# A staged fp32 transformer block on one core: in its ball stage the spread of reciprocal row sums goes to the end of a step, column scalings go to ScalarE, and a widening copy goes to GpSimd

## The reference

```python
def plin(x, w, b):                 # linear map between ball points
    return expmap0(logmap0(x) @ w + b)

xm = expmap0(layer_norm(logmap0(x)) * (1 + sc_msa) + sh_msa)
q, k, v = heads(plin(xm, w_q, b_q)), ...          # 16 heads of 16
attn = softmax(q @ k.T / sqrt(16))
attn_out = plin(from_heads(expmap0(attn @ v)), w_o, b_o)
x = mobius_add(residual, expmap0(g_msa * logmap0(attn_out)))
xm = expmap0(layer_norm(logmap0(x)) * (1 + sc_mlp) + sh_mlp)
ff = plin(plin(xm, w_f1, b_f1), w_f2, b_f2)       # 256 -> 1024 -> 256
out = mobius_add(x, expmap0(g_mlp * logmap0(ff)))
```

## Time and profile before

| what | us |
|---|---|
| median of 3 runs (range) | 3740.58 (3738.3 to 3744.46) |
| the profiled execution: its own time | 3737.99 |
| its span, first to last instruction | 3736.2 |
| stage 1, up to | 1205 |
| ball stage | 1205 to 2213 |
| of it, attention (first to last scores) | 1280.6 to 2067 |
| stage 3 | 2213 to 3736 |

### The profile page before, as it was taken

How to read it: one execution, slowest core, us unless ns; L and a number is a source line. 1 busy time by engine, 2 the same in 40 slices (tenths; PEclk the granted TensorE clock), 3 DMA queues, 4 the chain that set the end, 5 groups by cost and what they waited for, 6 DMA issues and landing times. The chain is left out here.

```text
span 3736.2 us, 51318 instructions
## 1 busy us (share of the span) xinstructions
PE 3404.0 (91%) x18088; PEld 1908.1 (51%) x18088; DVE 2195.9 (59%) x6472; ACT 1645.3 (44%) x3155; POOL 378.1 (10%) x234
## 2 busy tenths in 40 slices
PE   8999999999984588988898758999999999999998
PEld 3555555555552233444444434555555555555554
DVE  3234333334344567677775647777777777777773
ACT  2333333333331255544445215655555555555552
POOL 0000000000001001111112211111111111111110
PEclk9999999999997799999999879999999999999999
DMA  4010110110002100000000030000000000000000
GB/s 164 33 57 32 38 57 32 37 60 29 32 12 88 38 5 8 9 13 14 12 9 12 11 127 17 23 21 21 20 21 21 21 23 26 26 27 28 21 27 20
DMA packets 77553, 120.48 MB, mean 32 GB/s; under 512 B 10313, under 2 KB 66532, under 8 KB 72050
## 3 DMA queue, kind: packets, MB, share of 16 engines
q1 hardware_dynamic: 77298, 117.20, 9.1%
HBM read 96.16 MB, written 16.83 MB: 30 GB/s over the span
## 5 line engine op out<-in xcount | busy, mean ns | idle before, releaser
L2569 PE MATMUL wps<-w_wqkv,w_hT 128*128 128x512 f32 x768 | 379.4, 618 | 3.1 <-DMA w_wo<-in_wwo 3.1
L2607 PE MATMUL wps<-w_xnT,w_w 128*128 128x512 f32 (+1 forms) x768 | 351.5, 598 | 24.5 <-DVE w_xnT L2432 20.3
L2191 POOL TENSOR_TENSOR w_rn<-w_n,w_mhalf 128x16 f32<-128x16 f32 x64 | 187.4, 2927 | 1096.9 <-DVE w_n L2369 1096.9
L2219 ACT ACTIVATE w_pr<-w_sm,w_nmx,w_rn 128x256 f32<-128x256 f32 (+1 forms) x512 | 286.4, 562 | 10.2 <-DVE w_nmx L2350 9.6
L603 PE MATMUL ps<-xT,rw 128*128 128x512 f32 x512 | 245.4, 602 | 0.0
L2607 PEld LDWEIGHTS wps<-w_xnT,w_w 128*128 128x128 f32 (+1 forms) x768 | 133.2, 178 | 217.3 <-issue 193.7
L619 PE MATMUL ps<-hid,rw 128*128 128x512 f32 x512 | 240.7, 592 | 0.0
L1290 ACT ACTIVATE bb_pr<-bb_ps 128x1024 f32<-128x1024 f32 x128 | 130.5, 1020 | 203.8 <-PE bb_ps L1800 203.5
L2206 ACT ACTIVATE w_pT<-wps 128x512 f32<-128x512 f32 (+1 forms) x128 | 69.6, 544 | 329.2 <-PE wps L2516 329.2
L2569 PEld LDWEIGHTS wps<-w_wqkv,w_hT 128*128 128x128 f32 x768 | 137.9, 193 | 132.8 <-issue 127.7
L2619 PE MATMUL wps<-w_w,w_h2T 128*128 128x256 f32 (+1 forms) x768 | 190.1, 392 | 1.8 <-issue 1.8
(11 more groups left out here) (318 smaller groups left out, 6594.3 us busy)
## 6 DMA issues: line engine op xcount, KB each, us to landing
rw<-in_ew SPq DMA_DIRECT2D x32, 1024.0 KB, 6.7
w_xa<-xs SPq DMA_DIRECT2D x16, 512.0 KB, 3.8
w_xin<-xs SPq DMA_DIRECT2D x64, 128.0 KB, 3.8
xT<-in_xT SPq DMA_DIRECT2D x8, 512.0 KB, 3.9
xres<-in_x SPq DMA_DIRECT2D x32, 128.0 KB, 2.2
x<-x1t SPq DMA_DIRECT2D x32, 128.0 KB, 1.7
b_x<-x SPq DMA_DIRECT2D x1, 4096.0 KB, 14.3
bb_mod<-ada SPq DMA_DIRECT2D x16, 256.0 KB, 3.2
```

The lines of the kernel that those rows point to most:

```text
L2191: g.tensor_tensor(rn[:, i % 2, t], n2[:, n % 2, 1], mhalf[:], ALU.pow).then_inc(nr_ok, 1)
L2219: ins = a.activation(pr[:, j, lo:], sm[:, j, lo:], ACT.Exp, bias=nmx[:, G % 2, j:j + 1], scale=rn[:, i % 2, t, h:h + 1], accum_out=rs[:, G ...
L2569: ins = te.matmul(to, hT[:, i % 2, k, t * P:(t + 1) * P], wqkv[:, i // B, k, s * 512:(s + 1) * 512], start=(k == 0), stop=(k == KD - 1))
L2607: ins = te.matmul(to[0:n], w1[:, i // B, k, lo:lo + n], xnT[:, k], start=(k == 0), stop=(k == KD - 1))
```

## The change

Four parts, all in the ball stage:

1. On TensorE the job "bc" (`spread`) moves from the head of its step's side jobs to their end, and `turn_rows2` ("fu0", "fu1") to just ahead of the hidden layer. `side_jobs` follows, so the jobs get other banks. VectorE's `divide` and `limit_heads` are each due one step later.
2. The widening of rcp into rcx leaves VectorE (L1514) for GpSimd, between the roots and the sums of its step.
3. The scaling of x by FX (L1570), of u2 (L1644) and of wb by FW (L1691) leave VectorE for ScalarE, as Copy with a scale per row, at the head of its steps 24, 32 and 55. New semaphores join them.
4. `applied` moves from step 24 to step 25; `result` is no longer halved and runs in step 56.

```diff
@@ side_jobs(G)
-                if group_due(G, 1) is not None:
-                    yield "bc", group_due(G, 1)
...
-                if at(G, 33) is not None:
-                    yield "fu0", at(G, 33)
-                    yield "fu1", at(G, 33)
                 if group_due(G, 0) is not None:
                     yield "pk", group_due(G, 0)
...
+                if at(G, 33) is not None:
+                    yield "fu0", at(G, 33)
+                    yield "fu1", at(G, 33)
                 if among(G, F1):
...
                 if among(G, F2):
                     yield f"y{among(G, F2)[1]}", among(G, F2)[0]
+                if group_due(G, 1) is not None:
+                    yield "bc", group_due(G, 1)
@@ sync
-                        sp.wait_ge(out_ok, 2 * b + 2)
+                        sp.wait_ge(out_ok, b + 1)
@@ gpsimd
+                def widened(gg):
+                    emptied(pool, "pk", gg)
+                    if gg:
+                        filled(pool, "bc", gg - 1)
+                    g.tensor_copy(rcx[:], rcp[:].unsqueeze(3).broadcast_to([P, NT, 4, W])).then_inc(rcp_ok, 1)
+
                 for G in STEPS:
                     for asked in roots_asked(G):
                         root(*asked)
+                    if group_due(G, 0) is not None:
+                        widened(group_due(G, 0))
@@ scalar
+                def scaled(out, by):
+                    return a.activation(out, out, ACT.Copy, scale=by)
+
+                def scaled_rows(b):
+                    act.wait_ge(fac1_ok, b + 1)
+                    for t in range(b * NT, b * NT + NT):
+                        ins = scaled(x[:, t], FX[:, t:t + 1])
+                    ins.then_inc(xscaled, 1)
+
+                def scaled_rows2(b):
+                    act.wait_ge(lim2_ok, b + 1)
+                    for t in range(NT):
+                        ins = scaled(u2[:, t], lim[:, 1, t:t + 1])
+                    ins.then_inc(us_ok, 1)
+
+                def scaled_update(b):
+                    act.wait_ge(fac2_ok, b + 1)
+                    for t in range(NT):
+                        ins = scaled(wb[:, t], FW[:, b * NT + t:b * NT + t + 1])
+                    ins.then_inc(wscaled, 1)
...
                         turned_rows(tile_due(G, 0))
+                    if at(G, 24) is not None:
+                        scaled_rows(at(G, 24))
+                    if at(G, 32) is not None:
+                        scaled_rows2(at(G, 32))
+                    if at(G, 55) is not None:
+                        scaled_update(at(G, 55))
@@ vector
                 def invert(gg):
                     filled(dve, "pk", gg)
+                    if gg:
+                        dve.wait_ge(rcp_ok, gg)
                     v.reciprocal(rcp[:], ...).then_inc(done("pk", gg), 1)
-                    emptied(dve, "pk", gg)
-                    if gg:
-                        filled(dve, "bc", gg - 1)
-                    v.tensor_copy(rcx[:], ...).then_inc(rcp_ok, 1)
@@ step_factors
-                    s.tt(c(21), c(3), c(19), ALU.mult)
+                    v.tensor_tensor(c(21), c(3), c(19), ALU.mult).then_inc(fac_ok, 1)
@@ applied
-                    for t in range(b * NT, b * NT + NT):
-                        n = ch.mark(v.tensor_scalar(x[:, t], x[:, t], FX[:, t:t + 1], None, ALU.mult))
-                    ch.wait(n)
+                    dve.wait_ge(xscaled, b + 1)
@@ limited_rows, now limit_rows2
-                    s.ts(lim[:, 1], answer("u2", b), C, 1.0, ALU.mult, ALU.min)
-                    for t in range(NT):
-                        ins = v.tensor_scalar(u2[:, t], u2[:, t], lim[:, 1, t:t + 1], None, ALU.mult)
-                    ins.then_inc(us_ok, 1)
+                    s.ts(lim[:, 1], answer("u2", b), C, None, ALU.mult)
+                    v.tensor_scalar(lim[:, 1], lim[:, 1], 1.0, None, ALU.min).then_inc(lim2_ok, 1)
@@ result
-                    for t in (2 * p, 2 * p + 1):
-                        c = b * NT + t
-                        n = ch.mark(v.tensor_scalar(wb[:, t], wb[:, t], FW[:, c:c + 1], None, ALU.mult))
-                    ch.wait(n)
-                    for t in (2 * p, 2 * p + 1):
+                    dve.wait_ge(wscaled, b + 1)
+                    for t in range(NT):
@@ vector's loop
-                    if tile_due(G, 4) is not None:
-                        limit_heads(tile_due(G, 4))
-                    if group_due(G, 1) is not None:
-                        divide(group_due(G, 1))
+                    if tile_due(G, 5) is not None:
+                        limit_heads(tile_due(G, 5))
+                    if group_due(G, 2) is not None:
+                        divide(group_due(G, 2))
...
-                    if at(G, 24) is not None:
-                        applied(at(G, 24))
                     if at(G, 25) is not None:
+                        applied(at(G, 25))
                         row_norms(at(G, 25))
...
-                    if at(G, 55) is not None:
-                        result(at(G, 55), 0)
                     if at(G, 56) is not None:
-                        result(at(G, 56), 1)
+                        result(at(G, 56))
@@ tensor's loop: spread(gg) after second(...), turn_rows2(b) after project(...)
```

More of the change, by code:

```diff
@@ L1076, in ball_block @@
             w2_ok, out_ok, st_x = sem("w2_ok"), sem("out_ok"), sem("st_x")
+            fac1_ok, fac2_ok, lim2_ok, xscaled, wscaled = (sem(n) for n in ("fac1_ok", "fac2_ok", "lim2_ok", "xscaled", "wscaled"))
             full = {k: sem(f"full{k}") for k in (5, 6, 7)}
@@ L1509, in invert @@
                     filled(dve, "pk", gg)
+                    if gg:
+                        dve.wait_ge(rcp_ok, gg)
                     v.reciprocal(rcp[:], bank("pk", gg)[:, 0:4 * NT].rearrange("p (t r) -> p t r", r=4)).then_inc(done("pk", gg), 1)
-                    emptied(dve, "pk", gg)
-                    if gg:
-                        filled(dve, "bc", gg - 1)
-                    v.tensor_copy(rcx[:], rcp[:].unsqueeze(3).broadcast_to([P, NT, 4, W])).then_inc(rcp_ok, 1)
                 def divide(gg):
@@ L1549, in step_length, with step_factors @@
                     s.tt(c(19), c(19), c(18), ALU.mult)
-                def step_factors(b, th_ok):
+                def step_factors(b, th_ok, fac_ok):
                     c = columns(b)
@@ L1639, in ask_rows2, with limit_rows2 @@
                     ask("u2", b, usq[:, 1], EPS * EPS)
-                def limited_rows(b):
-                    s.ts(lim[:, 1], answer("u2", b), C, 1.0, ALU.mult, ALU.min)
-                    for t in range(NT):
-                        ins = v.tensor_scalar(u2[:, t], u2[:, t], lim[:, 1, t:t + 1], None, ALU.mult)
-                    ins.then_inc(us_ok, 1)
+                def limit_rows2(b):
+                    s.ts(lim[:, 1], answer("u2", b), C, None, ALU.mult)
+                    v.tensor_scalar(lim[:, 1], lim[:, 1], 1.0, None, ALU.min).then_inc(lim2_ok, 1)
                 def turned_rows2(b):
@@ L1686, in output_rows, with result @@
                                                    op0=ALU.mult, op1=ALU.add, accum_out=XW[:, c:c + 1]))
-                def result(b, p):
-                    for t in (2 * p, 2 * p + 1):
-                        c = b * NT + t
-                        n = ch.mark(v.tensor_scalar(wb[:, t], wb[:, t], FW[:, c:c + 1], None, ALU.mult))
-                    ch.wait(n)
-                    for t in (2 * p, 2 * p + 1):
+                def result(b):
+                    dve.wait_ge(wscaled, b + 1)
+                    for t in range(NT):
                         c = b * NT + t
@@ L1723, in _ @@
                     if at(G, 23) is not None:
-                        step_factors(at(G, 23), th1_ok)
-                    if at(G, 24) is not None:
-                        applied(at(G, 24))
+                        step_factors(at(G, 23), th1_ok, fac1_ok)
                     if at(G, 25) is not None:
+                        applied(at(G, 25))
                         row_norms(at(G, 25))
@@ L1740, in _ @@
                     if at(G, 32) is not None:
-                        limited_rows(at(G, 32))
+                        limit_rows2(at(G, 32))
                     if at(G, 52) is not None:
@@ L1746, in _ @@
                     if at(G, 54) is not None:
-                        step_factors(at(G, 54), th2_ok)
-                    if at(G, 55) is not None:
-                        result(at(G, 55), 0)
+                        step_factors(at(G, 54), th2_ok, fac2_ok)
                     if at(G, 56) is not None:
-                        result(at(G, 56), 1)
+                        result(at(G, 56))
                     if at(G, -23) is not None:
@@ L1903, in _ @@
                         heads(tile_due(G, 1), "v", 2 * D, 3 * D)
-                    if group_due(G, 1) is not None:
-                        spread(group_due(G, 1))
                     if tile_due(G, 7) is not None:
@@ L1909, in _ @@
                         turn_rows(tile_due(G, 0))
```

(6 more changed lines are left out.)

## The result

| | us |
|---|---|
| before, median of 4 runs | 3740.34 (3738.30 to 3744.46) |
| after, median of 4 runs | 3720.95 (3717.79 to 3722.32) |
| ratio | 0.9948, 95% interval 0.9936 to 0.9961 |
| the profiled execution of after; its span | 3720.94; 3719.2 |

What follows compares the result with a forecast made beforehand. VectorE, late at certain moments and the bound between the kT copies of steps 7 and 11, sets the pace; gains in full and later batches and drain less losses in batch 1 and light steps total 19.5: 3738.0 to 3718 us, range 3697 to 3738.

Steps and rivals of the forecast that it cites:

- The move alone is worth 1.0 of the 5.47 us: Step 9 of a full batch: moving the spread last saves 1.0 us; the rest must come from an earlier VectorE.
- Credit of a full batch, 4.55 us: Full batch: 3.8 us spared on VectorE plus 1.45 of step 13 less 0.7 for later jobs; three give 13.7.
- Term (b): VectorE, full batch: the first step factors move up by limit_heads and then wait for ScalarE's Tanh, 0.7 us back.
- (a): Full batch: 1.67 of x's 2.80 us, lost beside GpSimd's sums, fall on what VectorE runs then instead.
- Term (c): The widening on GpSimd takes 0.61 us there, of which VectorE loses 0.5.
- The divide: Standing behind ask_heads, it delays the projection, 3.6 us in batch 1, and turn_rows in a light step, 1.2 us.
- rival B: Slower: divide behind ask_heads delays turn_rows and six more projections, 43 us, giving 3761 us; chance 0.13.
- Batch 6: The batch whose spread wait ends at 1944 us, a weaker form of the full batches: gain of about 4 us.
- batch 7 with the drain: The last batch and the drain, up to stage 3: gain of 8.3 us.
- 2.8 for the drain: Drain: TensorE's waits of 8.13 and 3.10 us shrink by 1.5 to 2.7 each, less exposed scalings and divide: 2.8 us.
- A: The wait only moves, from the spread to qk's bank, VectorE in effect not relieved: 2 us, 3736 us; chance 0.17.
- C: More gain: the loss beside GpSimd does not return, 10 us, and the clock stays up: 3700 us; chance 0.20.

Runs made afterwards that it cites:

- e2: The kernel before with the offload alone: widening on GpSimd, scalings of x, u2 and wb on ScalarE, order and due steps as before; 3715.5 us.
- e3: The changed kernel with divide back in the step of its spread, ahead of ask_heads, except where a y job stands ahead of the spread; 3711.0 us.
- e11: The changed kernel with GpSimd's sums of hidden squares adding 8 of 512 columns only, all instructions and waits kept; 3682.8 us.
- e1: The kernel before with the moves alone: spread and turning of u2 last, limit_heads and divide a step later, nothing offloaded from VectorE; 3739.4 us.
- e4: The changed kernel with the widening of the reciprocals back on VectorE; 3718.5 us.
- e10: The changed kernel with divide back in its spread's step, and the scaling of u2 and the widening back on VectorE; 3704.9 us.
- e9: The changed kernel with divide back in its spread's step, u2's scaling back on VectorE and limit_heads back in its earlier step; 3704.9 us.
- e5: The changed kernel with the scaling of x back on VectorE, in the step where the kernel before had it; 3731.5 us.

## Why the prediction was right, and where it was not

**What bounds the kernel** was read rightly: VectorE between the kT copies of steps 7 and 11. They came 3.73 us closer in the changed kernel (30.39 beside 34.12; "some 4 us" forecast, 3.8 in the sum). In e2 and e3, with quite different orders on TensorE, batches 3 to 5 take 327.6 and 327.8 us, and in e11 VectorE's 3.35 us come back whole in the stretch: the pace is VectorE's.

**The spread.** No wait is left, and the new one of f4 for qk's bank is 3.33 us where 1 to 3 were forecast. "The move alone is worth 1.0 of the 5.47 us" was too kind: in e1 it is worth less than nothing in that step. The 1.45 us of step 13 did go.

**Credit of a full batch, 4.55 us**: 4.1, 4.4 and 2.9 measured, 11.4 instead of 13.7 for three. Term (b), 0.7 us, is there as a wait of 0.67 for the Tanh. The loss beside GpSimd did come back, as (a) had it, but the step erred on who pays: not "what VectorE runs then" among fused operations but limit_heads, and with 3.6 us in all, where before 2.6 were lost. Term (c), 0.5 lost against 0.47 gained, was 0.27 against 0.43; that the two come to no difference is confirmed by e4 and e10.

**limit_heads and divide a step later.** The divide was the danger, and where it was placed: batch 1 lost 3.7 us (4 forecast), batch 2 1.4 (0), batch 0 0.8. The fallen clock behind the projection's wait, 1.8 us in batch 1 and 2.9 in batch 2, was in no term. turn_rows waits 1.32 us in light steps (1.2 forecast), and for oT in steps 7 and 11 of full batches. No projection wait over 0.5 us in a full batch: rival B stays out.

**ScalarE's scalings** take 1.70 us for four of 128x256 (1.6 forecast), and TensorE's waits for the Exps did not grow (20.9 us in all, 23.4 before).

**Batch 6**, 9.1 instead of 4, and **batch 7 with the drain**, 4.9 instead of 8.3, are the mis-sized terms. In batch 6 both parts help: e1 and e2 each take 5.4 to 5.5 us off it alone, which the sum had as a small full batch. Why one adds to the other is open. In the last stretch the two terms were off in opposite ways. Batch 7, from its second scores to its last, gained 6.7 us (76.4 to 69.7) where 5.5 were forecast. "2.8 for the drain" failed: from the last scores to stage 3 it took 148.0 instead of 146.2 us, a loss of 1.8. Of the two waits that were to shrink by 1.5 to 2.7 us each, that of 8.13 did, to 6.45. That of 3.10 came back as two, of 1.54 and 1.75. The exposed scalings cost what they were priced at or a little more, 0.77 us in the wait for u2 and 0.4 at the end. And the clock, which no term had, fell behind that wait: the same matmuls took 3.5 us longer than in e2, whose drain takes 142.1 us, 4.2 less than before.

**The rivals.** A is refuted for the change and true for its moves. C is refuted by the trace of the changed kernel and by e9: the loss does return. (e5 lies nearer to the theory than to C.) Its price was the best hint in the text, though: e11 shows that the sums, the cause, cost 38 us with their own time.

## What to carry to other kernels

When an engine's time is stretched beside another's, moving the stretched operation away doesn't win the stretch: here the next one in line paid, however small it was, and of the kernels tried only the one with less work on GpSimd's side got the time back. A job moved one step later is priced by what it then stands behind: here a chain of small operations of 4 us, in the light batches where nothing else hides it. And a reordering that has no effect alone can cost on top of a change that does: test each half by itself.

## What the runs showed of the hardware that was not expected

An operation of VectorE on 128x48 elements takes 1.21 us instead of 0.21 when it meets a GpSimd sum of 1.35 us. In all four rows of the changed kernel the operation ends within 0.1 us of the sum, so the price there is the sum's rest, whatever the size of the operation. And matmuls behind a wait of the same length (3.71 us) ran at a granted clock of 0.62 in one kernel and 1.00 in another, 2.8 us apart over the same 24 instructions.
